# Attention stage: GpSimd weighs the fourth value row, gathers issued after both sums, ScalarE normalising half a pair later

## What is computed

```python
x = x + xattn(layernorm(x), ctx, seg_id, Wq, Wkv, Wo)
x = x + ffn(layernorm(x), w_gate, w_up, w_down)
# xattn: every token looks at 4 rows of the context
gather = seg_id[:, :, None] - arange(4)          # the token's row and the three before it
scores = einsum('bhqd,bhqkd->bhqk', q, k_sel) * HDIM ** -0.5
probs = softmax(where(gather < 0, neg_inf, scores))
out = einsum('bhqk,bhqkd->bhqd', probs, v_sel)   # the four value rows, weighed and summed
```

## Time and profile before

| | |
|---|---|
| median of 3 runs | 2551.17 us (2550.24 to 2552.89) |
| the profiled execution | 2549.47 us |
| its span in the trace | 2547.6 us |
| mean granted TensorE clock | 0.916 of 2.4 GHz |
| busy over the span | PE 80%, DVE 71%, ACT 54%, POOL 16% |
| attention stage | about 121 to 736 us |

### The profile page before, as it was taken

How to read it: one execution, slowest core, us unless ns; L and a number is a source line. 1 busy time by engine, 2 the same in 40 slices (tenths; PEclk the granted TensorE clock), 3 DMA queues, 4 the chain that set the end, 5 groups by cost and what they waited for, 6 DMA issues and landing times. The chain is left out here.

```text
span 2547.6 us, 25242 instructions
## 1 busy us (share of the span) xinstructions
PE 2028.6 (80%) x9560; PEld 948.8 (37%) x9560; DVE 1800.6 (71%) x1497; ACT 1366.1 (54%) x1434; POOL 420.2 (16%) x342
## 2 busy tenths in 40 slices
PE   4278888888749999999799999998000099999999
PEld 2134444444324444444344444443000044444444
DVE  8689999999924444442288888877699764678642
ACT  2536666666532222222288888543599753577530
POOL 0247767667620000000000000000000000000000
PEclk9589999999979999999899999999555599999999
DMA  7588888888434864854499997466799666555551
GB/s 266 205 365 332 313 336 316 322 329 310 191 152 152 260 234 163 264 194 151 163 322 347 344 348 267 190 239 232 307 374 364 270 257 226 199 210 211 226 234 66
DMA packets 143944, 652.94 MB, mean 256 GB/s; under 512 B 12496, under 2 KB 13008, under 8 KB 104016
## 3 DMA queue, kind: packets, MB, share of 16 engines
q1 hardware_dynamic: 133856, 514.49, 54.9%
q0 software_dynamic: 9216, 134.22, 13.6%
q10 hardware_dynamic: 752, 2.62, 0.3%
HBM read 452.71 MB, written 198.57 MB: 256 GB/s over the span
## 5 line engine op out<-in xcount | busy, mean ns | idle before, releaser
L1560 PE MATMUL fo_py<-kept_down,kept_gate 128*128 128x512 f16 x1536 | 458.4, 380 | 262.0 <-DVE kept_up L1542 262.0
L1264 PE MATMUL up_pp<-up_ah,kept_up 128*128 128x512 f16 x1536 | 463.0, 383 | 23.3 <-DVE up_al L1156 15.3
L983 PE MATMUL ga_pp<-ga_ah,kept_gate 128*128 128x512 f16 x1536 | 458.3, 380 | 18.0 <-DVE ga_al L888 18.0
L928 DVE TENSOR_REDUCE kept_gate_peak<-ga_raw 128x1 f32<-128x2048 f32 x48 | 109.7, 2285 | 298.3 <-ACT ga_raw L969 298.3
L1560 PEld LDWEIGHTS fo_py<-kept_down,kept_gate 128*128 128x128 f16 x1536 | 150.5, 98 | 444.5 <-DVE kept_up L1542 262.5
L1264 PE MATMUL up_pp<-up_al,kept_up 128*128 128x512 f16 x768 | 293.7, 382 | 0.0
L983 PE MATMUL ga_pp<-ga_al,kept_gate 128*128 128x512 f16 x768 | 291.8, 380 | 0.0
L1560 PE MATMUL fo_py<-kept_down,kept_up 128*128 128x512 f16 x768 | 291.8, 380 | 0.0
L969 ACT ACTIVATE ga_raw<-ga_pp 128x1024 f32<-128x1024 f32 x96 | 97.8, 1021 | 317.9 <-PE ga_pp L983 317.9
L626 POOL TENSOR_TENSOR at_kv_rows<-at_kv_rows 128x1024 f32<-128x1024 f32 x64 | 215.0, 3360 | 159.0 <-DVE at_kv_rows L562 157.8
L1264 PEld LDWEIGHTS up_pp<-up_ah,kept_up 128*128 128x128 f16 x1536 | 151.5, 99 | 210.3 <-DVE up_al L1156 16.3
(11 more groups left out here) (210 smaller groups left out, 3356.6 us busy)
## 6 DMA issues: line engine op xcount, KB each, us to landing
gate_scratch<-ga_raw SPq DMA_DIRECT2D x48, 1024.0 KB, 4.9
up_gin<-gate_scratch SPq DMA_DIRECT2D x48, 1024.0 KB, 9.0
up_scratch<-kept_up_raw SPq DMA_DIRECT2D x48, 1024.0 KB, 9.9
fo_ui<-up_scratch SPq DMA_DIRECT2D x48, 1024.0 KB, 9.0
pp_ui<-up_scratch SPq DMA_DIRECT2D x45, 1024.0 KB, 7.2
gate_integers<-up_gq SPq DMA_DIRECT2D x60, 512.0 KB, 9.3
kept_up<-gate_integers SPq DMA_DIRECT2D x48, 512.0 KB, 6.8
fo_gi<-gate_integers SPq DMA_DIRECT2D x48, 512.0 KB, 6.6
```

The source lines that it names most:

```text
L928: nc.vector.tensor_reduce(keep["gate_peak"][:, n:n + 1], raw[:, q, :], AX.X, ALU.max, apply_absolute_value=True).then_inc(m["peak"], 1)
L983: mm = nc.tensor.matmul(pp[k % 4][:, h, :], wt[w][:, c, f:f + P], a[:, b % 2, :, c, :], start=(q == 0), stop=(q == len(todo) - 1))
L1264: mm = nc.tensor.matmul(pp[k % 4][:, h, :], wt[w][:, c, f:f + P], a[:, b % 2, :, c, :], start=(q == 0), stop=(q == len(todo) - 1))
L1560: mm = nc.tensor.matmul(py[k % 8][:, :], a[b % 2][:, f, t * P:(t + 1) * P], wt[w][:, f, :], start=(q == 0 and i == 0), stop=(q == UNITS - ...
```

## The change

GpSimd multiplies the fourth value row (W - 1) of a tile with its weights, and VectorE only the first three. GpSimd starts a tile once both tiles of the pair are weighed by VectorE. It does multiply, sum, sum for the one tile, the same for the other, then both gathers, then `norm`. VectorE waits before it writes `pr` until GpSimd has used the old one. ScalarE (and PE with it) handles `normalise` and `take_hT` one tile later than before, and the exponential comes ahead of `take_ahi`.

```diff
@@ act
-                    if tile(2 * s_ - 8):
-                        take_hT(2 * s_ - 8)
+                    if tile(2 * s_ - 9):
+                        take_hT(2 * s_ - 9)
...
-                    if tile(2 * s_ - 7):
-                        normalise(2 * s_ - 7)
+                    if tile(2 * s_ - 8):
+                        normalise(2 * s_ - 8)
...
-                    if tile(2 * s_ - 2):
-                        take_ahi(2 * s_ - 2)
                     if pair(s_):
                         act.wait_ge(m["ds"], s_ + 1)
                         need(act, m["pr"], s_)
                         nc.scalar.activation(ex[:, :, :, :], ds[:, :, :, :], ACT.Exp).then_inc(m["ex"], 1)
-                    if tile(2 * s_ - 6):
-                        normalise(2 * s_ - 6)
+                    if tile(2 * s_ - 2):
+                        take_ahi(2 * s_ - 2)
+                    if tile(2 * s_ - 7):
+                        normalise(2 * s_ - 7)
...
-                    if tile(2 * s_ - 7):
-                        take_hT(2 * s_ - 7)
+                    if tile(2 * s_ - 8):
+                        take_hT(2 * s_ - 8)
@@ vector: weigh, and ahead of pr
-                    values = kv[:, t % KR, :, D:2 * D].rearrange("p w (h e) -> p w h e", h=H)
-                    nc.vector.tensor_tensor(values, values, pr[:, t % 2].unsqueeze(3).to_broadcast([P, W, H, HD]),
+                    values = kv[:, t % KR, 0:W - 1, D:2 * D].rearrange("p w (h e) -> p w h e", h=H)
+                    nc.vector.tensor_tensor(values, values, pr[:, t % 2, 0:W - 1].unsqueeze(3).to_broadcast([P, W - 1, H, HD]),
                                             ALU.mult).then_inc(m["pv"], 1)
...
+                        need(dve, m["last"], a)
@@ gpsimd
                 def add_up(t):
+                    last = kv[:, t % KR, W - 1, D:2 * D].rearrange("p (h e) -> p h e", h=H)
                     lower, upper = kv[:, t % KR, 0:2, D:2 * D], kv[:, t % KR, 2:4, D:2 * D]
-                    pool.wait_ge(m["pv"], t + 1)
+                    pool.wait_ge(rows_in[t % KR], 16 * (t // KR + 1))
+                    pool.wait_ge(m["pr"], t // 2 + 1)
+                    pool.wait_ge(m["pv"], t // 2 * 2 + 2)
+                    nc.gpsimd.tensor_tensor(last, last, pr[:, t % 2, W - 1].unsqueeze(2).to_broadcast([P, H, HD]),
+                                            ALU.mult).then_inc(m["last"], 1)
+                    pool.wait_ge(m["last"], t + 1)
                     nc.gpsimd.tensor_tensor(lower, lower, upper, ALU.add).then_inc(m["half"], 1)
...
+                def gather_next(t):
                     pool.wait_ge(m["att"], t + 1)
                     gather(t + KR)
...
                         add_up(2 * s_ - 2)
                         add_up(2 * s_ - 1)
+                        gather_next(2 * s_ - 2)
+                        gather_next(2 * s_ - 1)
```

More of the change, by code:

```diff
@@ L408, in attention @@
         rows_in = [s.sem(f"rows_in{i}") for i in range(KR)]
-        m = s.sems("xn xT xhi xrest xlo q prod raw sc top ds ex tot inv pr pv half att aT ahi arest alo o x1 "
+        m = s.sems("xn xT xhi xrest xlo q prod raw sc top ds ex tot inv pr pv last half att aT ahi arest alo o x1 "
                    "nmean ssq sqe root rstd norm hn hT hT_sb peak consts reduced")
@@ L719, in _ @@
                         rest_a(2 * s_ - 3)
-                    if tile(2 * s_ - 8):
-                        turn_h(2 * s_ - 8)
+                    if tile(2 * s_ - 9):
+                        turn_h(2 * s_ - 9)
                     if pair(s_ + 1):
@@ L733, in _ @@
                         rest_a(2 * s_ - 2)
-                    if tile(2 * s_ - 7):
-                        turn_h(2 * s_ - 7)
+                    if tile(2 * s_ - 8):
+                        turn_h(2 * s_ - 8)
                     if tile(2 * s_ - 2):
```

## The result

The changed kernel takes 2516.43 us (median of 4 runs, 2515.36 to 2516.73) against 2551.63 us before: 0.9861 of the time, interval 0.9844 to 0.9879, 35.2 us less. The profiled execution took 2515.36 us with a span of 2513.5. That is outside my range of 2522 to 2564, on the fast side.

A forecast was written before the change was run, and what follows sets the result against it. DVE was taken as the bound, busy 98.9 of 100 us in the attention. Weighing -34.1, collision +24.8 and end of the stage -4 gave -13.3 us, in round 2538 us; range 2522 to 2564.

The forecast's parts named there:

- The weighing: DVE's weighing in the attention falls from 2048 to 1536 elements for each partition, 64 x 0.53 us: -34.1 us.
- Multiplying 512 elements: POOL's new multiplication, priced like a sum of 512 at 1.28 us, with 2.37 us as the upper bound.
- The prediction's last sentence: Wrong above all if POOL's multiplication with its repeated input costs something else than a sum; every POOL mark counts it twice.
- The collision: POOL's second `att` holds DVE's `sc` 0.59 us, plus 0.2 us for `norm`; 0.8 us in each of 31 pairs: +24.8 us.
- `norm`: POOL's `norm` falls on DVE's `pr` and weighing, estimated at 0.1 us each for two of its instructions.
- Rival 3: `norm` holds DVE for its whole length, 0.5 us more a pair: +15.5, 2553 us; chance 0.10.
- rival 1: POOL does not hold DVE's small two-input instructions, so all of the weighing is gained: -34.1 - 4, 2513 us; chance 0.12.
- The gathers: POOL's gathers, moved to about T+10.6 and T+11.9 (T: DVE's first product of a pair), still land in time: cost nothing.
- ScalarE: Earlier exponential and later `hn` give 0 in the pairs; waits for POOL's `norm` at the stage's end go: -4 us.

The follow-up runs named there:

- e1: The changed kernel, with GpSimd multiplying the fourth value row by the third value row instead of by the weights repeated over each head; 2530.62 us.
- e6: The changed kernel, with VectorE's second residual of a slot done before the mask instruction `sc` instead of after `ds`; 2510.42 us.
- e4: The changed kernel, with `normalise`, `take_hT` and TensorE's `turn_h` back at the tiles of the kernel before; 2531.96 us.
- e2: The changed kernel, with the first tile's gather back between the two tiles' sums; 2537.55 us.
- e3: The changed kernel, with GpSimd waiting for its own tile's weighing only, not for that of both tiles; 2511.33 us.

## Why the prediction was wrong

- **The weighing, -34.1 us.** Right: 1756 ns where I had 1755.
- **"Multiplying 512 elements ... so I take 1.28 ... below 1.28 I see no reason."** This is the step that failed. It is 1.05 us, because one of its inputs is repeated over a head; e1 shows it, with 1.28 for a full input. It counts twice ahead of the second `att`, 0.46 us. Two smaller errors of the same paragraph cancel: POOL starts at T+0.26 and not at T+0.15, and the second multiplication begins 0.05 us ahead of the end of the first `att` (it waits for nothing that `att` makes) and not behind it. With the price of 1.28, in e1, the second `att` ends at T+10.36, and the forecast had T+10.35. I took 1.28 from the nearest row as if it were a lower bound and looked only upward for the uncertainty. The prediction's last sentence names this price as its weakest point, yet no rival has it cheaper.
- **The collision, +24.8 us.** The mechanism was right, the size was not. `att` ended at T+9.91 and not at T+10.35, and the overlap with `sc` was 0.14 and not 0.59 us: 6.3 us in all. I had 31 x 0.59 = 18.3 us for `sc`. A difference of 0.44 us on an engine that isn't the bound decided about 14 us of the result, by e1 against the changed kernel. With the assumption put in (e1) the kernel takes 2530.6 us; the forecast of 2538 had 6.2 us more, for `norm`.
- **`norm`, 0.2 us a pair in it.** Measured nothing. Rival 3, the rule at its word, falls with it: in e6 `pr` came 0.38 us before the end of `root` and was not held. About the Trainium skill's rule ("SBUF — State Buffer", "Who interferes with whom"): the trace agrees for instructions on hundreds of elements, in both directions, and for `shift`, on two elements, which the weighing holds (1.64 us). It does not for `root`, on two elements, which runs beside `ds` and `pr` and holds neither (0.29 us). That the weighing would hold `norm` I had not seen; in e4 ACT waits for just that.
- **No collision (rival 1, 2513 us).** Its time came out within 3.5 us, its reason didn't: e1, e2 and the first pairs show DVE held for 0.6 to 0.8 us.
- **The gathers, 0.** Right: DVE waits for one gather, in the first pair, as before, though their median landing rose from 10.6 to 12.7 us. The token loads took 14.3 us to land in the median, where I had reckoned with the 3.6 of before; the ring of eight pairs covered that too.
- **ScalarE, 0 in the middle and -4 at the end.** Right in sum (4.65). What I had not seen is that the shift was needed: without it (e4) the kernel is about 15 us slower.

## What to carry to other kernels

When work moves from the bounding engine to one that can hold it up, as GpSimd and VectorE hold each other here, lay both timelines over each other with times to a tenth of a microsecond, and ask which instruction of the bounding engine, however small, falls into the other's long ones, and which of the other's falls into the bounding engine's. If the answer hangs on a few tenths, the forecast is two numbers and not one; take a price without a row from both sides. And look for the remedy before giving up the move: an instruction with one SBUF input put ahead of the one that is held, or a helper that starts earlier, gave 5 to 6 us each here.

## What the runs showed of the hardware

- A GpSimd multiplication with an input repeated over 32 elements takes 1.05 us for 512 elements and 1.91 for 1024; with two full inputs 1.28 us for 512, as the sum does, which takes 2.37 for 1024. In each extra element that is 1.69 ns against 2.13.
- A DVE instruction held by GpSimd goes on 0.2 us before the recorded end of GpSimd's (0.21 after the change, 0.20 in e1). A GpSimd instruction that was already issued and held by a weighing starts 0.05 to 0.07 us ahead of DVE's next instruction (the sum of before, the multiplication of e3), one that waits for its semaphore 0.26 us behind it (after).
- A GpSimd instruction on two elements that is held by a DVE instruction passes between two of DVE's that follow each other without a gap, and DVE's 3.43 us for both don't change (after, e6). Whether a long one would do so no run shows.
- `root`, 0.72 us on two elements, does not hold the DVE instructions with two SBUF inputs that begin beside it: `ds` in the kernel before and `pr` in e6 take 0.29 us. GpSimd's `att`, 1.27 us on 512 elements, does hold them (`ds` 0.90 us in e2).
